# A router-gated expert layer and a two-way state scan on one core: two accumulations start from a ScalarE copy instead of an identity product

## The chip, the core and the metric

The kernel runs on one core of a Trainium2 chip. Its time is the device time of one execution in microseconds (us); the smaller, the better. The core has five instruction streams that run side by side and meet at semaphores: PE (TensorE, products into PSUM banks), DVE (VectorE), ACT (ScalarE), POOL (GpSimd) and SP (SyncE, here the queue that issues every transfer).

## What is computed

Eight images of 96 channels and 4096 pixels go through two layers, all in 32-bit floats. The reference, cut to what matters:

```python
# layer 0: four experts, two of them gated per pixel
gates = softmax(top2(tokens @ router_w.T + router_b))          # zero for the other two
for ei in range(4):
    hid = gelu(tokens @ fc1_w[ei].T + fc1_b[ei])
    out = out + gates[..., ei:ei + 1] * (hid @ fc2_w[ei].T + fc2_b[ei])
x2 = x + scale[0] * out

# layer 1: normalise over channels, then a selective scan over the pixels, forwards and backwards
x_norm = (x2 - mean) * rsqrt(var + 1e-5) * gamma + beta
def mamba(u):
    xr, z = split(u @ W_in);  xr = silu(conv4(xr) + conv_b)
    dt, B, C = split(xr @ W_xproj);  dt = softplus(dt @ W_dt + b_dt)
    h_t = exp(dt_t * A) * h_(t-1) + (dt_t * xr_t) * B_t        # 192 channels x 16 states
    y_t = sum_n(h_t * C_t) + xr * D
    return (y * silu(z)) @ W_out
out = 0.5 * (mamba(x_norm) + mamba(x_norm reversed) reversed) + x2
```

## The kernel before

**Tiling.** An image is cut into 8 chunks of 512 pixels. The 192 x 16 states of a chunk are 24 tiles of 128 rows, in six batches of four. After a setup, one *body* works on one chunk in one direction: 8 forward bodies and then 8 reverse ones for each image, 128 in all. The text calls them F0 to F7 and R0 to R7; R0 works on the last chunk again, from its right end. The even bodies also carry half of the expert layer's work of one piece (512 pixels) of the *next* image, the odd ones the other half.

**One body on the engines.** DVE runs 24 scans (line 1180, one for each tile, each on its factor exp(dt A)), four products with B (1164), the gated hidden tiles (1144, three of them, at scans 14, 15 and 16) and the products of the summed state with silu(z), called *gated y* below (1185). ACT computes the 24 factors (944) into a ring of three PSUM banks, two tiles ahead of DVE; so it can be at most three ahead. In between it has the softplus, gelu, silu and copy steps, at fixed tile numbers. POOL multiplies each scanned batch by C (1267) and two batches by B (1257). PE sums the states of each batch into the bank of y (`sum_states`, 710) and does all projections. Every engine's order is written out by hand in its `body`; nothing is reordered.

**The bank of y.** y is summed in one PSUM bank in two parts, *low* (batches 0 and 1) and *high* (batches 2 to 5). Each part opens with ACT writing xr D into the bank (`seed`, 949). In a reverse body PE then adds the forward y of the same chunk by a product with the identity (704, `y_begin`) and the result passes gate and output projection. The high sum of body n ends in body n + 1: PE there adds batches 4 and 5, and DVE takes the gated y (1185) ahead of its scan 6. The low one is taken at scan 13.

**The forward y** of a chunk is copied out of PSUM by ACT into `yf` (`evacuate`, 954), stored to memory (526) and loaded back into `yb` (531) for the reverse body. For R0 this is a round trip through memory directly after the forward pass: `yf` low is copied in F7, `yf` high at tile 5 of R0.

**The two sums that start from x.** "Y2" is the second expert layer's output in work bank 0: in an even body PE adds x by an identity product (652, `residual`) and six products with the hidden tiles (658) and three for the bias (662). "OUT" is the chunk's output in work bank 1: PE adds x2 by an identity product (719, `finish`) and two products with the gated y (720, 721). It happens one body after each reverse body, so in R1 to R7 and in F0 (`fin` in the code).

**SP's queue** is in order: a wait holds all issues behind it. In a body it waits for "D1" (the softplus input projection), loads the window of the chunk two ahead (439), the residual x2 (521), stores and loads B and C (451, 463, 470), stores and loads dt and dt x (445, 446, 476, 456, 481), and in an even body loads x of the next piece (423), for which it waits until Y2 is complete.

## Time and profile before

| what | value |
|---|---|
| median of 3 runs | 6012.41 us (5996.08 to 6017.89) |
| the profiled execution, its own time | 6026.74 us |
| its span, first instruction to last | 6024.9 us |
| DVE busy in it | 5274.0 us, 88% |
| POOL busy | 5153.9 us, 86% |
| PE busy | 4725.7 us, 78% |
| ACT busy | 4472.2 us, 74% |
| mean granted TensorE clock | 0.84 of full speed |

The first scan begins at 401.5 us and the last ends at 6007.2 us of the span, so a body takes 43.8 us in the mean; what comes before is the router, the gates and the first image's experts. No engine is saturated: DVE and POOL hand batches to each other and each waits for the other, and DVE waits for factors, for sums and for gate rows. So the profile is read body by body, where one begins at its first scan.

### The profile page before, as it was taken

The numbers are of one execution on the slowest core, as the hardware profiler recorded it, in microseconds if no ns is written. First come the engines' busy times: TensorE is split into PE (matmuls) and PEld (weight loads), VectorE is DVE, ScalarE is ACT, GpSimd is POOL, SyncE is SP. The second block draws the span as 40 slices with busy tenths as digits, with TensorE's granted clock in tenths as the row PEclk, the third lists the DMA queues.
The fourth block names the chain that finished last, engine by engine and source line by source line (L and its number), as shares of the span: only waits on it lengthen the run. The fifth ranks groups of instructions, "written<-read, shape, count | busy, mean of one in ns | idle before, by whom it ended". The sixth has DMA issues, their size and how long they took to land.

```text
span 6024.9 us, 68387 instructions
## 1 busy us (share of the span) xinstructions
PE 4725.7 (78%) x13769; PEld 1472.7 (24%) x13769; DVE 5274.0 (88%) x4473; ACT 4472.2 (74%) x6727; POOL 5153.9 (86%) x2127
## 2 busy tenths in 40 slices
PE   7767788777887778777787778777787778877787
PEld 7222222222222222222222222222222222222222
DVE  1239989998999989999899989999899998999898
ACT  0448877787777877778777877778777787778776
POOL 0039988999899989999899988999899998999898
PEclk9877788878887878877888788888888878887788
DMA  3046667676776766676676766666676766766776
GB/s 95 22 99 164 169 163 174 164 172 161 173 169 163 173 157 172 167 170 162 169 178 161 173 160 171 167 172 163 169 170 163 175 161 166 172 168 165 169 177 149
DMA packets 428352, 964.89 MB, mean 160 GB/s; under 512 B 58081, under 2 KB 58330, under 8 KB 394985
## 3 DMA queue, kind: packets, MB, share of 16 engines
q1 hardware_dynamic: 428008, 961.31, 65.4%
q14 instruction: 249, 2.03, 0.1%
q8 instruction: 95, 1.56, 0.1%
HBM read 776.98 MB, written 184.11 MB: 160 GB/s over the span
## 4 chain that ended last, share of the span: by engine, by line
issue 22%; DVE 19%; PE 18%; ACT 12%; DMA 11%; POOL 7%; SPq 2%; DVEq 1%; ACTq 1%; POOLq 0%
DVE X L1180 13%; PE ps L679 5%; DMA bc_d<-bc 4%; POOL X L1267 4%; DVE X L1164 4%; ACT ps L944 3%; PE ps L710 3%; POOL X L1257 2%; DMA lo_d<-bc 2%; DMA lo<-lo_d 2%; PE ps L658 2%; DVE hid L1144 2%; PE ps L694 1%; DMA y_d<-yf 1%; PE ps L684 1%
## 5 line engine op out<-in xcount | busy, mean ns | idle before, releaser
L1267 POOL TENSOR_TENSOR X<-X,cR 128x2048 f32<-128x2048 f32 x768 | 3477.8, 4528 | 61.7
L1180 DVE TENSOR_TENSOR_SCAN X<-ps,carry,X 128x512 f32<-128x512 f32 x2688 | 3258.5, 1260 | 113.3 <-ACT ps L944 91.5
L944 ACT ACTIVATE ps<-hi,amat 128x512 f32<-128x512 f32 x2048 | 1375.1, 682 | 688.0 <-DVE X L1180 684.6
L1164 DVE TENSOR_TENSOR X<-hi,ps 128x2048 f32<-128x2048 f32 x512 | 1158.9, 2264 | 85.2 <-PE ps L710 81.9
L710 PE MATMUL ps<-X,red 128*32 128x512 f32 x6144 | 918.0, 673 | 377.3 <-POOL X L1267 376.8
L1257 POOL TENSOR_TENSOR X<-lo,bR 128x2048 f32<-128x2048 f32 x258 | 1167.4, 4525 | 40.0 <-DMA lo<-lo_d 38.6
L679 PE MATMUL ps<-win,w_u 97*128 97x512 f32 (+1 forms) x2080 | 1118.5, 688 | 11.6 <-DMA win<-xn_d 8.6
L944 ACT ACTIVATE ps<-lo,amat 128x512 f32<-128x512 f32 x1026 | 687.3, 677 | 165.1 <-DVE X L1180 132.0
L694 PE MATMUL ps<-xr,wd 128*96 128x512 f32 (+1 forms) x520 | 417.8, 898 | 340.7 <-ACT xr L899 287.6
L642 PE MATMUL ps<-xp,w 96*128 96x512 f32 x864 | 534.2, 754 | 67.4 <-DMA xp<-in_x 67.1
L679 PEld LDWEIGHTS ps<-win,w_u 97*128 97x128 f32 (+1 forms) x2080 | 372.3, 190 | 652.2 <-issue 637.6
L1180 DVE TENSOR_TENSOR_SCAN X<-ps,X 128x512 f32<-128x512 f32 x384 | 445.3, 1202 | 38.3 <-POOL X L1257 18.9
L1144 DVE TENSOR_TENSOR hid<-ps,hid 128x512 f32<-128x512 f32 x432 | 287.4, 667 | 210.7 <-PE ps L649 210.1
L1265 POOL COPY carry<-X 128x4 f32<-128x4 f32 x768 | 143.2, 187 | 359.1 <-DVE X L1180 354.6
L658 PE MATMUL ps<-hid,w 128*96 128x512 f32 x852 | 421.3, 615 | 0.0
L710 PEld LDWEIGHTS ps<-X,red 128*32 128x32 f32 x6144 | 125.5, 112 | 1067.2 <-POOL X L1267 660.7
L695 PE MATMUL ps<-xr,wd 65*96 65x512 f32 (+1 forms) x520 | 373.2, 809 | 0.0
L1230 POOL TENSOR_TENSOR xnp<-xc,sq 96x512 f32<-96x512 f32 x71 | 90.1, 1269 | 330.5 <-ACT sq L892 330.5
L857 ACT ACT_TABLE_LOAD x265 | 340.0, 1283 | 4.7
L866 ACT ACTIVATE hid<-ps,b 128x512 f32<-128x512 f32 x432 | 273.3, 685 | 61.1 <-PE ps L642 59.0
L932 ACT ACTIVATE ps<-bR 128x512 f32<-128x512 f32 x512 | 298.1, 582 | 0.0
L642 PEld LDWEIGHTS ps<-xp,w 96*128 96x128 f32 x864 | 185.9, 234 | 413.5 <-issue 377.7
(112 smaller groups left out, 4291.9 us busy)
## 6 DMA issues: line engine op xcount, KB each, us to landing
hi<-hi_d SPq DMA_DIRECT2D x516, 512.0 KB, 8.5
bR<-bc_d SPq DMA_DIRECT2D x516, 256.0 KB, 4.5
lo<-lo_d SPq DMA_DIRECT2D x516, 256.0 KB, 4.6
cR<-bc_d SPq DMA_DIRECT2D x516, 256.0 KB, 6.9
hi_d<-S SPq DMA_DIRECT2D x258, 256.0 KB, 7.8
y_d<-yf SPq DMA_DIRECT2D x128, 256.0 KB, 8.4
yb<-y_d SPq DMA_DIRECT2D x128, 256.0 KB, 7.6
win<-xn_d SPq DMA_DIRECT2D x130, 196.3 KB
```

The costliest lines, as they stand in the source:

```text
L642: ready(u, f"H{m}", mm(begin(u, f"H{m}")[:, :], w1[:, P * m:P * m + P], xp[:, :], start=True, stop=True))
L658: mm(p_w[u.at["Y2"][0]][0:C, :], w2[:, m, :], hid[:, m, :], start=False, stop=False)
L679: last = mm(out[0:m, :], w_u[:, t, a:a + m], win[:, par, at:at + CH], start=(t == 0), stop=(t == TAPS - 1))
L694: mm(out[0:m, :], w_d[0][:, a:a + m], xr[0][:, par, :], start=True, stop=False)
L695: ready(u, name, mm(out[0:m, :], w_d[1][:, a:a + m], xr[1][0:DR + 1, par, :], start=False, stop=True))
L710: last = mm(p_y[GRP * j:GRP * j + GRP, :], red[:, :], X[:, slot(par, s), j, :], start=False, stop=(s in (LOW - 1, NB - 1)), skip_group_che ...
L944: A_(p_a[i % RING][:, :], dt, ACT.Exp, scale=amat[:, column(i):column(i) + 1]).then_inc(s_exp, 1)
L1144: free(u, f"G{m}", V.tensor_tensor(hid[:, m, :], begin(u, f"G{m}")[:, :], hid[:, m, :], ALU.mult))
L1164: V.tensor_tensor(X[:, slot(par, s), :, :], hi[:, par, HIGH:2 * HIGH, :], p_b[:, :].unsqueeze(1).to_broadcast([P, BATCH, CH]), ALU.mult).t ...
L1180: V.tensor_tensor_scan(h, a, h, 0.0 if head else carry[:, i:i + 1], ALU.mult, ALU.add).then_inc(s_scan, 1)
L1257: G.tensor_tensor(batch(par, s), lo[:, LOW:2 * LOW, :].unsqueeze(1).to_broadcast([P, 2, 2, CH]), quads(bR, par, s), ALU.mult).then_inc(s_b ...
L1267: G.tensor_tensor(batch(par, s), batch(par, s), quads(cR, par, s), ALU.mult).then_inc(s_hc, 1)
```

## The change

- `residual` is gone from the body (it stays in the setup loop). ACT writes x from `xp` into the bank of Y2 (`seed_x`) right behind its factor of tile 2, ahead of the softplus; the products with the hidden tiles accumulate onto it.
- The identity product of `finish` is gone but for the very last chunk. ACT writes x2 from `xf` into the bank of OUT (`seed_out`) at tile 6, behind the seed of y and ahead of the copy of Y2.
- In an even body PE sums the batches 4 and 5 of the body before directly behind one another, and the last three products of the second expert layer come behind both. Batch 2 is summed ahead of the second projection (`project(1)`), in even bodies only.
- R0 takes the forward y out of `yf`, where ACT wrote it, and the last chunk's two loads of `yb` are dropped. That chunk is still stored.
- SP's load of the next piece's x waits for `seed_x`, no longer for a complete Y2.

```diff
@@ SP @@
                 if not odd:
-                    bank, at = u.at["Y2"]
-                    wait_alone(s_pr[bank], at + 1)
+                    wait_alone(s_xs, pc - NCH + 1)
                     load_piece(nimg, j)
...
                 if before == 0:
                     store_y(0, n - 1, NCH - 1 if rev else q * 2 + odd - 1)
-                    if rev:
-                        load_y(0, (img + 1) * NCH, NCH - 1, n * NB + (LOW + 2))
...
-                if nrev:
-                    following = NCH - 1 if not rev else chunk_of(q, rev, odd) - 1
-                    load_y(1, (img + 1) * NCH, following, n * NB + (NB + 1))
+                if nrev and rev:
+                    load_y(1, (img + 1) * NCH, chunk_of(q, rev, odd) - 1, n * NB + (NB + 1))
@@ PE @@
-            def y_begin(low, n, f, par):
+            def y_begin(low, n, first, f, par):
                 pe.wait_ge(s_seed, n * 2 + (1 if low else 2))
-                if f is not None:
-                    pe.wait_ge(s_yl[low], f * 16 + 16)
-                    mm(p_y[:, :], ident[:, :], yb[:, low, :], start=False, stop=False, skip_group_check=True)
+                if f is not None or first:
+                    src = yf if first else yb
+                    if not first:
+                        pe.wait_ge(s_yl[low], f * 16)
+                    mm(p_y[:, :], ident[:, :], src[:, low, :], start=False, stop=False, skip_group_check=True)
...
                 pe.wait_ge(s_ev, n * 2 + 4)
-                pe.wait_ge(s_xf, f * 16 + 16)
-                out = begin(u, "OUT") if u is not None else p_b
-                mm(out[0:C, :], ident[0:C, 0:C], xf[:, :], start=True, stop=False)
+                if u is not None:
+                    out = begin(u, "OUT")
+                    pe.wait_ge(s_fs, f + 1)
+                else:
+                    out = p_b
+                    pe.wait_ge(s_xf, f * 16 + 16)
+                    mm(out[0:C, :], ident[0:C, 0:C], xf[:, :], start=True, stop=False, skip_group_check=True)
...
-                    residual(u)
+                    begin(u, "Y2")
+                    pe.wait_ge(s_xs, pc - NCH + 1)
                     for m in range(3):
                         expert_out(m, u, None)
                     if before is not None:
                         sum_states(n - 1, NB - 2, nxt)
-                    expert_out(3, u, None)
-                    expert_out(4, u, None)
-                    if before is not None:
                         sum_states(n - 1, NB - 1, nxt)
-                    expert_out(5, u, None)
+                    for m in range(3, HT):
+                        expert_out(m, u, None)
                     expert_bias(u)
-                y_begin(1, n, f, par)
+                y_begin(1, n, first, f, par)
...
-                y_begin(0, n, f, par)
+                y_begin(0, n, first, f, par)
+                if not odd:
+                    sum_states(n, 2, par)
                 project(1, par, urev, u)
-                sum_states(n, 2, par)
+                if odd:
+                    sum_states(n, 2, par)
@@ ACT @@
+            def seed_x(v, pc):
+                bank, at = v.at["Y2"]
+                act.wait_ge(s_pf[bank], at + 1)
+                act.wait_ge(s_xp, pc * 16)
+                A_(p_w[bank][0:C, :], xp[:, :], ACT.Copy).then_inc(s_xs, 1)
+
+            def seed_out(u, f):
+                bank, at = u.at["OUT"]
+                act.wait_ge(s_pf[bank], at + 1)
+                act.wait_ge(s_xf, f * 16 + 16)
+                A_(p_w[bank][0:C, :], xf[:, :], ACT.Copy).then_inc(s_fs, 1)
...
                     if i == 0:
+                        if not odd:
+                            seed_x(u, pc)
                         softplus_start(1, u, n + 1)
...
-                    if i == 6 and not odd:
-                        copy_x2(u, pc - 1)
+                    if i == 6:
+                        if before == 1:
+                            seed_out(u, finished(img, q, rev, odd)[2])
+                        if not odd:
+                            copy_x2(u, pc - 1)
```

PE at the head of the even bodies R2 and R4 (one loop), before: x by the identity, three hidden tiles, then the two late sums with two hidden tiles between them.

```order
L652 MATMUL ps<-xp,ident 96x512
L658 MATMUL ps<-hid,w 96x512 x3
...
L710 MATMUL ps<-X,red 32x512 x4
L658 MATMUL ps<-hid,w 96x512 x2
...
L710 MATMUL ps<-X,red 32x512 x4
L658 MATMUL ps<-hid,w 96x512
L662 MATMUL ps<-gT,b2s 96x512 x3
```

The same place of the changed kernel (lines shifted: 652 was the identity product, 656 is 658, 711 is 710, 660 is 662).

```order
L656 MATMUL ps<-hid,w 96x512 x3
L709 ISA
L711 MATMUL ps<-X,red 32x512 x4
L709 REGISTER_ALU
L711 MATMUL ps<-X,red 32x512 x4
L656 MATMUL ps<-hid,w 96x512 x3
L660 MATMUL ps<-gT,b2s 96x512 x3
```

The identity product is gone and the second late sum stands ahead of two hidden products that it stood behind.

SP between the last body of a forward pass and the loads of R0, before: the store of the low forward y (526) and its load (531) stand ahead of R0's window (439).

```order
L526 DMA y_d<-yf 128x512
L387 ISA
L387 REGISTER_ALU
L531 DMA yb<-y_d 128x512
L387 REGISTER_ALU
L439 ISA
L439 DMA win<-xn_d 97x518
L387 REGISTER_ALU
L451 DMA bc_d<-bc 32x512
```

And of the changed kernel (528 is 526, 441 is 439, 453 is 451).

```order
L528 DMA y_d<-yf 128x512
L389 REGISTER_ALU
L441 ISA
L441 DMA win<-xn_d 97x518
L389 REGISTER_ALU
L453 DMA bc_d<-bc 32x512
```

R0's window and its store of B and C are no longer behind a load that waits for a store to land.

## Rows read from the trace of the kernel before

**Rows 1.** The page's head: span, and busy time, share and instructions of each engine.

```profile
span 6024.9 us, 68387 instructions
PE 4725.7 (78%) x13769; PEld 1472.7 (24%) x13769; DVE 5274.0 (88%) x4473; ACT 4472.2 (74%) x6727; POOL 5153.9 (86%) x2127
```

**Rows 2.** Waits of DVE, whole span: who <- whom: us in total, times, longest.

```profile
DVE hid L1144 <- PE ps L649: 210.1, 86, 16.4
DVE yr L1185 <- PE ps L710: 128.6, 50, 9.3
DVE X L1180 <- ACT ps L944: 110.1, 137, 2.4
...
DVE X L1164 <- PE ps L710: 81.9, 61, 8.9
```

**Rows 3.** Sums over stretches: length, busy by engine, means. All R0; then R2, R4, R6.

```profile
sum 423.80, PE 342.47 PEld 100.50 DVE 316.81 ACT 289.00 POOL 331.11; mean PE 42.81 PEld 12.56 DVE 39.60 ACT 36.12 POOL 41.39
...
sum 1089.80, PE 989.21 PEld 303.89 DVE 996.96 ACT 862.64 POOL 963.09; mean PE 41.22 PEld 12.66 DVE 41.54 ACT 35.94 POOL 40.13
```

**Rows 4.** Timeline of R0, image 5: start, us, what [idle before it <- who ended it].

```profile
3549.59 0.27 SPq L439 DMA_DIRECT2D win<-xn_d  x1
...
3559.90 1.71 SPq L463 DMA_DIRECT2D bR<-bc_d  x4
...
3563.17 0.34 SPq L423 DMA_DIRECT2D xp<-in_x  x1
...
3569.18 4.53 PE L642 MATMUL ps<-xp,w 96*128 96x512 f32 x6 [4.01 <-DMA xp<-in_x]
...
3574.78 0.69 DVE L1185 TENSOR_TENSOR yr<-ps,sz 128x512 f32<-128x512 f32 x1 [4.50 <-PE ps L710]
...
3585.80 2.05 PE L704 MATMUL ps<-yb,ident 128*128 128x512 f32 x2 [6.61 <-DMA yb<-y_d]
...
3593.77 2.29 DVE L1164 TENSOR_TENSOR X<-hi,ps 128x2048 f32<-128x2048 f32 x1 [7.61 <-PE ps L710]
```

**Rows 5.** Waits of PE for transfers, whole span.

```profile
PE ps L642 <- DMA xp<-in_x: 67.1, 31, 6.6
...
PE ps L704 <- DMA yb<-y_d: 41.1, 8, 6.6
```

**Rows 6.** Timeline at the head of R4, image 4, whose first scan is at 3032.4.

```profile
3033.57 4.55 POOL L1267 TENSOR_TENSOR X<-X,cR 128x2048 f32<-128x2048 f32 x1
...
3035.64 1.10 PE L652 MATMUL ps<-xp,ident 96*96 96x512 f32 x2
...
3040.25 1.96 PE L658 MATMUL ps<-hid,w 128*96 128x512 f32 x4
3042.13 1.07 PE L710 MATMUL ps<-X,red 128*32 128x512 f32 x8
...
3043.27 0.69 DVE L1185 TENSOR_TENSOR yr<-ps,sz 128x512 f32<-128x512 f32 x1 [2.54 <-PE ps L710]
```

**Rows 7.** Stretches: R2 and R4 of image 5 (length, busy, granted clock, DMA, GB/s).

```profile
3645.60:3691.30 45.70, 38.86 (x109) 11.75 (x108) 41.36 (x36) 36.00 (x55) 41.41 (x18) 0.87 0.69 170
3734.80:3778.30 43.50, 37.55 (x110) 11.48 (x109) 41.42 (x36) 35.88 (x55) 41.34 (x18) 0.92 0.72 182
```

**Rows 8.** PE and DVE in these two bodies, timeline.

```profile
3664.13 4.18 PE L642 MATMUL ps<-xp,w 96*128 96x512 f32 x6 [1.84 <-DMA xp<-in_x]
...
3669.68 0.69 DVE L1185 TENSOR_TENSOR yr<-ps,sz 128x512 f32<-128x512 f32 x1 [2.54 <-PE ps L710]
...
3752.60 2.84 PE L642 MATMUL ps<-xp,w 96*128 96x512 f32 x6 [1.14 <-DMA xp<-in_x]
...
3756.50 0.69 DVE L1185 TENSOR_TENSOR yr<-ps,sz 128x512 f32<-128x512 f32 x1 [0.19 <-PE ps L710]
```

**Rows 9.** ACT and DVE at the head of R4, image 4, timeline.

```profile
3037.71 2.44 DVE L1180 TENSOR_TENSOR_SCAN X<-ps,carry,X 128x512 f32<-128x512 f32 x2
...
3038.02 0.67 ACT L944 ACTIVATE ps<-lo,amat 128x512 f32<-128x512 f32 x1
```

**Rows 10.** Group by shape: busy, mean ns | idle. Then a transfer: KB, median us.

```profile
L932 ACT ACTIVATE ps<-bR 128x512 f32<-128x512 f32 x512 | 298.1, 582 | 0.0
...
xf<-x_d SPq DMA_DIRECT2D x64, 192.0 KB, 10.1
```

More of the change, by code:

```diff
@@ L340, in moe_mamba @@
         s_seed = sem("y_seeded")
+        s_xs = sem("x_seeded")
+        s_fs = sem("residual_seeded")
         s_ys = [sem("forward_y_high_stored"), sem("forward_y_low_stored")]
@@ L591, in _ @@
                 sp.wait_ge(s_win[k], 16 * (IMGS * BODIES // 2 + 1))
-                sp.wait_ge(s_yl[k], 16 * NCH * IMGS)
+                sp.wait_ge(s_yl[k], 16 * (NCH - 1) * IMGS)
             for replicated in (s_lo, s_hi, s_b, s_c):
@@ L651, in residual @@
             def residual(u):
[L652 removed]
+                mm(begin(u, "Y2")[0:C, :], ident[0:C, 0:C], xp[:, :], start=True, stop=False, skip_group_check=True)
             def expert_out(m, u, gu):
@@ L657, in expert_out @@
                     pe.wait_ge(s_pf[bank], at + 2)
-                mm(p_w[u.at["Y2"][0]][0:C, :], w2[:, m, :], hid[:, m, :], start=False, stop=False)
+                mm(p_w[u.at["Y2"][0]][0:C, :], w2[:, m, :], hid[:, m, :], start=False, stop=False, skip_group_check=True)
             def expert_bias(u):
                 for s in range(3):
-                    last = mm(p_w[u.at["Y2"][0]][0:C, :], b2s[:, s, :], gT[:, :], start=False, stop=(s == 2))
+                    last = mm(p_w[u.at["Y2"][0]][0:C, :], b2s[:, s, :], gT[:, :], start=False, stop=(s == 2), skip_group_check=True)
                 ready(u, "Y2", last)
@@ L716, in finish @@
                 pe.wait_ge(s_ev, n * 2 + 4)
-                pe.wait_ge(s_xf, f * 16 + 16)
-                out = begin(u, "OUT") if u is not None else p_b
-                mm(out[0:C, :], ident[0:C, 0:C], xf[:, :], start=True, stop=False)
-                mm(out[0:C, :], wo0[:, :], yr0[:, :], start=False, stop=False)
-                last = mm(out[0:C, :], wo1[:, :], yr1[:, par, :], start=False, stop=True)
+                if u is not None:
[5 more added lines that the diff above has]
+                    mm(out[0:C, :], ident[0:C, 0:C], xf[:, :], start=True, stop=False, skip_group_check=True)
+                mm(out[0:C, :], wo0[:, :], yr0[:, :], start=False, stop=False, skip_group_check=True)
+                last = mm(out[0:C, :], wo1[:, :], yr1[:, par, :], start=False, stop=True, skip_group_check=True)
                 if u is not None:
@@ L771, in body @@
                 nimg = next_image(img)
-                f = img * NCH + q * 2 + odd if rev else None
+                first = rev == 1 and before == 0
+                f = img * (NCH - 1) + q * 2 + odd if rev and not first else None
                 windows = (img * (BODIES // 2) + q + ((NCH // 2) * rev + 2)) * 16
```

1 line of the change is left out of this document (removed).

## The prediction

> **What bounds the kernel now.** I read the page's head first [rows 1]: DVE is busy 88% and POOL 86%, so neither is full and the time lies in what DVE waits for. The waits of DVE [rows 2] name three that the change touches: the gated y waits for PE's sums (128.6 us in 50 times), the product with B waits for PE to have summed the slot that it overwrites (81.9 in 61), the gated hidden tile waits for a gate row (210.1 in 86). Then I cut the span into bodies and summed them by kind [rows 3]. The 8 bodies R0 take 423.8 / 8 = 53.0 us each, and DVE works in 39.6 of them: 13.4 us idle. The 24 bodies R2, R4 and R6 take 1089.8 / 24 = 45.4 each with 41.5 of work: 3.9 idle. The mean body is 43.8. R0 is the outlier, and its timeline [rows 4] shows why in two places. PE stands 4.01 us for x of the next piece, and DVE then 4.50 for the low sum behind it. Then PE stands 6.61 us for the forward y on its way through memory, runs its product at half speed (2.05 us), and DVE waits 7.61. The waits of PE [rows 5] hold 8 such waits for yb, 41.1 us: one for each image. In the even reverse bodies it is the high sum [rows 6]: DVE waits 2.54 us for it at the gated y, while POOL's last product of the old body had ended at 3033.57 + 4.55 = 3038.12, 4 us before PE came to sum it at 3042.13. PE is late there, by its own work.
>
> **The change part by part.**
>
> *R0's forward y from `yf`.* PE's product at 3585.80 no longer waits: its data lie in SBUF from tile 5 of the body on, and the seed that it also needs waits for no transfer. DVE's 7.61 us go. Over the 8 images PE waited 5.1 in the mean and 6.61 here, while DVE waited 1.0 more than PE; that bounds DVE's mean by 6.1 and 7.6, and the longest wait of this kind is 8.9 [rows 2, 5]. I take 7.0: 8 x 7.0 = 56 us. What is late next is ACT: behind its silu steps the factors come late, in 110.1 / 137 = 0.8 us a time [rows 2], a wait that R0 now meets as the other reverse bodies do: 8 x 0.8 = 6 back. Net **-50 us**, bounds -40 and -60. Batch 2 is also summed ahead of the second projection; the slot is then free earlier, but ACT's silu is what DVE waits for next, so this counts nothing.
>
> *R0's two loads and their waits on SP.* A load of yb that had to wait for its store stood ahead of R0's window. From the window's issue to the landing of B and C's store, which lets 463 go, it is 3559.90 - 3549.59 = 10.3 us, and x of the next piece is issued 3.3 us behind that and comes 6.0 us later [rows 4]. So as much as the window moves forward, x does, and DVE's 4.50 shrinks by that. No row shows how long SP stood for the store; the bounds are 0 and PE's 4.0 us. I take 1.5, nearer to the lower one since the projection that frees the window ends late too: 8 x 1.5 = **-12 us**, bounds 0 and -32.
>
> *Even reverse bodies: the identity product of x, and the sum moved ahead.* On PE's path to the high sum the change takes out 1.10 us (652) and puts 1.96 us (658) behind it: 3.06 us. The sum would end at 3043.20 - 3.06 = 3040.14, and DVE is there at 3043.27 - 2.54 = 3040.73 [rows 6]. The wait of 2.54 goes wholly. What is late next can be seen in two bodies of image 5 in which PE happened to come early and the gated y had no wait at tile 6: R4 took 43.5 us and R2 took 45.7 [rows 7]. In both PE then stood for x of the next piece. In R4 it was 1.14 us, the six products took 2.84, and the low sum cost DVE 0.19. In R2 it was 1.84 us, the products took 4.18, part of them at the lower clock, and DVE waited 2.54 for the low sum: the whole gain was lost one step on [rows 8]. So a body is worth between -0.3 (45.4 - 45.7) and +1.9 us (45.4 - 43.5). SP issues the load of x behind the stores of dt, not behind Y2, so its new wait moves nothing, and x lands as late as before. PE comes there another 1.0 us earlier, since the identity product of x2 is gone as well, which makes its stand longer. I take three bodies of R4's sort for one of R2's: (3 x 1.9 - 0.3) / 4 = 1.35.
>
> *The copies on ACT.* Their price: the copy SBUF to PSUM of 512 columns is 582 ns [rows 10]. At the head of a body ACT is dense. Scan 5 starts at 3037.71 + 1.22 = 3038.93 and its factor is ready at 3038.69 [rows 9]: 0.24 us of cover, so of the 0.58 of `seed_x` 0.34 lands on DVE. That leaves 1.0 in an even reverse body: 24 x 1.0 = **-24 us**, bounds -46 and +15 (45.7 + 0.34 - 45.4 = 0.64 each). The store of B and C is 0.58 us later too, but it lands behind the window and the residual (10.1 us) anyway. In F2, F4 and F6 the 0.34 has no gain beside it, and waits for gate rows at tile 14 hide a part: 0 to 0.34, I take 0.3: 24 x 0.3 = **+7 us**. `seed_out` stands at tile 6, behind the seed of y; the residual comes 10.1 us after its issue [rows 10], which is about when ACT gets there, so ACT may stand up to 1 us. Queued behind it are the copy of Y2 and the factor of tile 9, and PE's products of OUT wait for it; DVE has a product with B (2.3 us, rows 4) and three scans of 1.2 ahead of that tile. I count nothing.
>
> *F0 and the odd bodies.* F0 loses its own wait for the high sum, and as in R2 of image 5 I expect x to give it back one step on: 0, bounds -1 and +1 a body (8 us either way). Odd reverse bodies have one product less (1.0 us) in a stretch in which PE waits for POOL: 0.
>
> *Sum:* 50 + 12 + 24 - 7 = 79 us. The profiled execution took 6026.7 and would take 5948; the median of the runs is 14 us lower, 6012.4, so the **forecast is 5933 us**, 1.3% faster.
>
> **The rivals.**
>
> *Everything lands* (0.15). x is early enough everywhere and the clock holds: R0 8 x (7.6 + 4.0) = 93, even reverse bodies 24 x 1.9 = 46: 139 us, 5873. For it: in R4 of image 5 it was so. Against it: R2 of the same image, and that nothing brings x earlier outside R0.
>
> *Only R0's round trip pays* (0.12). The even reverse bodies trade the wait for the high sum for one for the low sum, and `seed_x` costs 0.34 us in all 56 other even bodies: 50 - 19 = 31 us, 5981. For it: R2 of image 5.
>
> *R0 pays by half* (0.07). With yb gone something else holds its second half, the high dt loads or ACT: 8 x 3.5 = 28 in place of 50, 5955.
>
> *TensorE at the lower clock; slower than before* (0.04). With two products out of its dense stretch PE idles longer ahead of the products with x. The granted clock was 0.92 in R4 and 0.87 in R2 of image 5, and the difference of these bodies is 45.7 - 43.5 = 2.2 us. If every even body goes R2's way, the 24 reverse ones lose 0.64 each (15 us) and the 32 forward ones 2.2 (70 us), against 50 from R0: 6012 + 35 = 6047. [...]
> The Trainium skill, "TensorE: Matmul & The Clock Gate", section "What's actually happening", says that the lower clock is the default state and activity releases it: a rule against taking products out of PE. By it alone the result would be the 6047 of this rival instead of 5933; the two bodies agree with its direction, and no row shows that all bodies would follow.
>
> **How the numbers follow.** The forecast has 0.62: its own range is 5905 to 5960. The rivals have 0.15, 0.12, 0.07 and 0.04. The range to hold 8 of 10 takes in most of the first and the second: 5880 to 5985. A measurement of this kernel can tell some 0.5% from no change, that is 30 us: faster below 5982, slower above 6042. Faster: 0.62 + 0.15 + 0.07 + half of 0.12 = 0.90; the other half of the second and a part of the last are within: 0.07; slower 0.03.
>
> **What the changed profile would show.** R0 near 44.5 us (from 53.0) with no wait of PE for yb, and DVE's wait for the low sum there at 3 us in place of 4 to 5. The gated y at tile 6 without a wait in R2, R4, R6 and F0. PE's wait for x longer in total than 67.1 us, in more than 31 places. The even reverse bodies in two sorts again, near 44 and near 46. DVE waiting for factors about 0.3 us at scan 5 of even bodies. The prediction is wrong if R0 stays above 48, if the bodies R2 to R6 stay at 45.4, or if the forward ones grow by over 1 us.

## The result, and the profile after

The changed kernel took 5920.86 us in the median of four runs (5911.16 to 5929.55), the kernel before 6014.51 beside it (5996.08 to 6017.89): a ratio of 0.985, interval 0.9825 to 0.9876. The forecast was 5933. The profiled execution has a span of 5920.9 us against 6024.9.

Line numbers move: the scan is 1208 (was 1180), the gated y 1213 (1185), the product with B 1192 (1164), the gated hidden tile 1172 (1144), the factor 967 (944), PE's sums 711 (710), its products with x of the next piece 640 (642). The waits of DVE over the whole span (who <- whom: us in total, times, longest), beside [rows 2]:

```profile
DVE hid L1172 <- PE ps L647: 213.0, 95, 17.3
DVE X L1208 <- ACT ps L967: 136.0, 164, 2.0
...
DVE yr L1213 <- PE ps L711: 74.1, 32, 9.3
...
DVE X L1192 <- PE ps L711: 10.4, 28, 0.4
```

The gated y fell from 128.6 to 74.1 us and the product with B from 81.9 to 10.4; waits for factors rose from 110.1 to 136.0. Of PE's two rows of waits for transfers in [rows 5] one is left (yb is gone), and it has grown from 67.1 us in 31 places:

```profile
PE ps L640 <- DMA xp<-in_x: 102.7, 61, 6.9
```

R0 of image 5, beside [rows 4]: SP's issues of the window, of B and C's store, of their load and of x, then PE's products with x, then the two waits of DVE of over 1 us that are left.

```profile
3492.99 0.26 SPq L441 DMA_DIRECT2D win<-xn_d  x1
3497.70 0.31 SPq L453 DMA_DIRECT2D bc_d<-bc  x1
3503.13 1.69 SPq L465 DMA_DIRECT2D bR<-bc_d  x4
...
3506.71 0.34 SPq L425 DMA_DIRECT2D xp<-in_x  x1
...
3512.00 5.49 PE L640 MATMUL ps<-xp,w 96*128 96x512 f32 x6 [3.26 <-DMA xp<-in_x]
...
3519.42 0.69 DVE L1213 TENSOR_TENSOR yr<-ps,sz 128x512 f32<-128x512 f32 x1 [4.67 <-PE ps L711]
...
3537.87 2.34 DVE L1208 TENSOR_TENSOR_SCAN X<-ps,X 128x512 f32<-128x512 f32 x2 [1.52 <-ACT ps L967]
```

The 7.61 us at the second product with B are gone; x is issued 12.8 us into the body (3506.71 - 3493.91) in place of 13.6, and DVE's 4.67 us for the low sum stand as before. In this image 5 is the exception. Over all eight R0, x is issued 13.1 us into the body in the mean in place of 14.7, and DVE's waits for the low sum add up to 30.4 us in place of 42.2. R0 of image 4, before and then changed:

```profile
2877.67 0.69 DVE L1185 TENSOR_TENSOR yr<-ps,sz 128x512 f32<-128x512 f32 x1 [7.02 <-PE ps L710]
...
2832.21 0.69 DVE L1213 TENSOR_TENSOR yr<-ps,sz 128x512 f32<-128x512 f32 x1 [3.49 <-PE ps L711]
```

Summed by kinds of bodies (a view of stretches: length, busy by engine, means): R0; then R2, R4, R6; then F2, F4, F6 and the odd forward bodies, and after them these last two of the kernel before.

```profile
sum 360.30, PE 308.31 PEld 93.55 DVE 315.44 ACT 291.96 POOL 320.42; mean PE 38.54 PEld 11.69 DVE 39.43 ACT 36.50 POOL 40.05
...
sum 1073.20, PE 934.44 PEld 282.77 DVE 995.81 ACT 887.17 POOL 978.25; mean PE 38.93 PEld 11.78 DVE 41.49 ACT 36.97 POOL 40.76
...
sum 988.10, PE 756.13 PEld 233.96 DVE 964.38 ACT 857.13 POOL 904.94; mean PE 31.51 PEld 9.75 DVE 40.18 ACT 35.71 POOL 37.71
...
sum 1376.00, PE 998.21 PEld 265.54 DVE 1289.23 ACT 1049.79 POOL 1353.69; mean PE 31.19 PEld 8.30 DVE 40.29 ACT 32.81 POOL 42.30
```

```profile
sum 1025.00, PE 832.10 PEld 252.83 DVE 967.02 ACT 850.03 POOL 943.70; mean PE 34.67 PEld 10.53 DVE 40.29 ACT 35.42 POOL 39.32
...
sum 1349.40, PE 964.89 PEld 258.50 DVE 1286.10 ACT 1046.80 POOL 1310.09; mean PE 30.15 PEld 8.08 DVE 40.19 ACT 32.71 POOL 40.94
```

With the sums of the other kinds from the same view:

| kind (count) | before | after | difference | forecast |
|---|---|---|---|---|
| R0 (8) | 423.8 | 360.3 | -63.5 | -62 |
| R2, R4, R6 (24) | 1089.8 | 1073.2 | -16.6 | -24 |
| R odd (32) | 1366.4 | 1359.1 | -7.3 | 0 |
| F0 (8) | 351.3 | 346.2 | -5.1 | 0 |
| F2, F4, F6 (24) | 1025.0 | 988.1 | -36.9 | +7 |
| F odd (32) | 1349.4 | 1376.0 | +26.6 | 0 |

So the reverse half went as forecast (-87 against -86). In the forward half two large differences that were not forecast nearly cancel (-15 in all).

The even reverse bodies R2, R4 and R6 come in two sorts, and the clock tells them apart. In 13 of the 24 PE's six products with x ran at a granted clock of 1.00 throughout (2.84 us); these bodies take 42.9 to 44.7 us, 43.8 in the mean. In 11 the clock over the products was 0.62 to 0.75 (3.70 to 4.49 us), so they ran in part at the lower level; these take 45.4 to 46.4, 45.8 in the mean. Before the change it was 1 of 24. R4 and R6 of image 5, which take 43.3 and 45.6 us, PE and then the stretch of its products:

```profile
3689.22 2.84 PE L640 MATMUL ps<-xp,w 96*128 96x512 f32 x6 [1.69 <-DMA xp<-in_x]
3689.20:3692.10 2.90, 2.88 (x10) 1.17 (x14) 2.90 (x3) 2.87 (x5) 0.73 (x3) 1.00 0.78 194
...
3775.34 3.90 PE L640 MATMUL ps<-xp,w 96*128 96x512 f32 x6 [1.78 <-DMA xp<-in_x]
3775.30:3779.20 3.90, 3.86 (x10) 1.24 (x12) 3.52 (x3) 3.27 (x5) 1.73 (x3) 0.71 0.91 214
```

The length of the stand ahead does not sort them by itself: PE had stood 0.14 to 2.37 us in the bodies at 1.00 and 1.56 to 2.58 us in the others.

The experiments ask what carries each part.

### The profile page after: what moved, and what is told of

Its sections match the earlier page's. It is cut to its first block, busy times and chain, and to the rows that moved or that the text cites. A ratio compares the mean times of both kernels' runs of the same rounds, so it can differ in the third digit from the quotient of the medians.

```text
span 5920.9 us, 68105 instructions
## 1 busy us (share of the span) xinstructions
PE 4658.8 (79%) x13515; PEld 1447.1 (24%) x13515; DVE 5270.1 (89%) x4473; ACT 4531.7 (77%) x6854; POOL 5155.7 (87%) x2127
## 4 chain that ended last, share of the span: by engine, by line
issue 23%; DVE 21%; PE 14%; DMA 12%; ACT 11%; POOL 7%; SPq 3%; DVEq 1%; ACTq 1%; POOLq 0%
DVE X L1208 14%; DMA bc_d<-bc 5%; PE ps L677 4%; DVE X L1192 4%; POOL X L1295 4%; ACT ps L967 3%; POOL X L1285 2%; DMA lo<-lo_d 2%; DMA xp<-in_x 2%; PE ps L711 2%; DMA lo_d<-bc 2%; PE ps L640 2%; DVE hid L1172 2%; PE ps L682 2%; SPq L465 1%
## 5 line engine op out<-in xcount | busy, mean ns | idle before, releaser
L1295 POOL TENSOR_TENSOR X<-X,cR 128x2048 f32<-128x2048 f32 x768 | 3477.9, 4529 | 62.2 <-POOL carry L1293 0.7
L1192 DVE TENSOR_TENSOR X<-hi,ps 128x2048 f32<-128x2048 f32 x512 | 1158.3, 2262 | 10.4 <-PE ps L711 10.4
L711 PE MATMUL ps<-X,red 128*32 128x512 f32 x6144 | 900.2, 666 | 334.1 <-POOL X L1295 331.0
L692 PE MATMUL ps<-xr,wd 128*96 128x512 f32 (+1 forms) x520 | 451.7, 967 | 334.4 <-ACT xr L922 281.3
L640 PE MATMUL ps<-xp,w 96*128 96x512 f32 x864 | 528.7, 746 | 104.2 <-DMA xp<-in_x 102.7
L1172 DVE TENSOR_TENSOR hid<-ps,hid 128x512 f32<-128x512 f32 x432 | 288.2, 669 | 213.4 <-PE ps L647 213.0
L693 PE MATMUL ps<-xr,wd 65*96 65x512 f32 (+1 forms) x520 | 400.3, 864 | 0.0
L682 PE MATMUL ps<-win,w_g 97*128 97x512 f32 x256 | 177.2, 780 | 156.0 <-ACT xr L922 156.0
```

What stands on the lines that cost most here:

```text
L640: ready(u, f"H{m}", mm(begin(u, f"H{m}")[:, :], w1[:, P * m:P * m + P], xp[:, :], start=True, stop=True))
L692: mm(out[0:m, :], w_d[0][:, a:a + m], xr[0][:, par, :], start=True, stop=False)
L693: ready(u, name, mm(out[0:m, :], w_d[1][:, a:a + m], xr[1][0:DR + 1, par, :], start=False, stop=True))
L711: last = mm(p_y[GRP * j:GRP * j + GRP, :], red[:, :], X[:, slot(par, s), j, :], start=False, stop=(s in (LOW - 1, NB - 1)), skip_group_che ...
L1172: free(u, f"G{m}", V.tensor_tensor(hid[:, m, :], begin(u, f"G{m}")[:, :], hid[:, m, :], ALU.mult))
L1192: V.tensor_tensor(X[:, slot(par, s), :, :], hi[:, par, HIGH:2 * HIGH, :], p_b[:, :].unsqueeze(1).to_broadcast([P, BATCH, CH]), ALU.mult).t ...
```

## The experiments

In the table, ratios are to the kernel before, run on the same chip each time; body lengths are from one profile each (sum of the kind by its count), and "forward" is the sum of all 64 forward bodies. A difference of under 1 us in the column of R2, R4 and R6 need not come from the edit: e8_pool touches forward bodies alone, and that column rose from 44.7 to 45.7.

| kernel | ratio (95%) | R0 | R2, 4, 6 | R odd | forward |
|---|---|---|---|---|---|
| before | 1 | 53.0 | 45.4 | 42.7 | 2726 |
| changed | 0.985 (0.9825 to 0.9876) | 45.0 | 44.7 | 42.5 | 2710 |
| e1_yf | 0.9894 (0.9868 to 0.992) | 45.7 | 44.6 | 42.9 | 2722 |
| e2_sums | 0.999 (0.998 to 1.0) | 52.2 | 44.5 | 43.0 | 2726 |
| e3_no_seed_x | 0.9858 (0.9829 to 0.9886) | 45.5 | 44.8 | 42.4 | 2721 |
| e4_no_seed_out | 0.9878 (0.9861 to 0.9894) | 46.3 | 44.4 | 43.2 | 2713 |
| e5_sum2_back | 0.988 (0.9857 to 0.9903) | 45.1 | 45.4 | 42.5 | 2723 |
| e6_x_early | 0.9785 (0.9765 to 0.9806) | 42.2 | 44.2 | 42.7 | 2706 |
| e7_fill | 0.9836 (0.9813 to 0.986) | 43.4 | 45.1 | 42.5 | 2726 |
| e8_pool | 0.986 (0.9835 to 0.9884) | 45.2 | 45.7 | 42.5 | 2701 |
| e9_pe_x | 0.9798 (0.9782 to 0.9814) | 42.6 | 44.2 | 42.5 | 2722 |
| e10_no_copies | 0.9844 (0.9827 to 0.986) | 43.8 | 44.7 | 43.0 | 2719 |
| e11_pe_x_pool | 0.9784 (0.9768 to 0.9801) | 42.5 | 44.1 | 42.5 | 2709 |
| e12_residual_first | 0.9923 (0.9909 to 0.9937) | 42.6 | 43.7 | 44.5 | 2736 |

**e1_yf: R0's forward y alone**

```diff
-                    if rev:
-                        load_y(0, (img + 1) * NCH, NCH - 1, n * NB + (LOW + 2))
...
-                    mm(p_y[:, :], ident[:, :], yb[:, low, :], start=False, ...)
+                    src = yf if first else yb
+                    mm(p_y[:, :], ident[:, :], src[:, low, :], start=False, ...)
```

> The kernel before with one part of the change alone: in R0 the forward y comes from yf, and the two loads of yb that R0 had per image are gone. Nothing else is touched. Theory A (the prediction's first two terms): R0 falls from 53.0 us to about 45 as in the changed kernel, 8 x 7.8 = 62 us, all other kinds of bodies stay within 0.3 us of the kernel before: 6014 - 62 = 5952. Rival B (R0's fall in the changed kernel also needs the earlier high sum and x2 out of PE): R0 stays at 47 or above, gain below 48 us, above 5966. Rival C (what R0 gains is handed to its neighbours): R0 near 45, R1 longer by 1 us or more.

Measured 5954 against 6024: 70 us, Theory A (forecast 5952). This one part is some 1.1 of the change's 1.5%. R0 lost 7.2 us. R2, R4 and R6 fell too, by 0.8 us each, to where the whole change has them, with both identity products and the old order of sums still in place. That was not expected by any theory. The waits left in them are not those of the changed kernel: DVE still waits for the high sum in 13 of these 24 bodies, 31.8 us in all (20 and 54.6 before, none in the changed kernel), and the clock over the products with x falls in 2 of them (11 in the changed kernel). That both have the same mean is not shown to have one cause.

**e2_sums: batch 5 summed directly behind batch 4, alone**

```diff
-                    expert_out(3, u, None)
-                    expert_out(4, u, None)
-                    if before is not None:
                         sum_states(n - 1, NB - 1, nxt)
-                    expert_out(5, u, None)
+                    for m in range(3, HT):
+                        expert_out(m, u, None)
```

> The kernel before with PE's sum of the last batch (5) put directly behind that of batch 4 in even bodies, ahead of products 3 and 4 of the second expert layer; both identity products stay on PE. By the trace of before that moves the high sum 1.96 us earlier. Theory A (the place of the sum carries what the change gains in even bodies outside R0): F2, F4 and F6 fall by 1.0 to 1.5 us a body (24 to 36 us), the even reverse bodies by 0.5 to 0.7 (12 to 17), the odd forward bodies grow by 0.5 to 0.8 (16 to 26) since POOL sets the length of a forward pair, and all in all 15 to 30 us go: 5985 to 6000. Rival B (the product taken out of PE carries it): less than 8 us, above 6006, and the wait of DVE at the gated y of tile 6 stays in more than half of the even bodies.

A miss for Theory A in time: 0.999. (The table's row flatters it: the profiled run, 6010 us, is one of the fastest of ten, which took 6009 to 6027.) The high sum does come earlier, and its wait goes from 128.6 us to 68.8, but the product with B takes most of it back: 81.9 became 100.6, and 3.1 us for ACT's copies of B became 20.2:

```profile
DVE X L1162 <- PE ps L710: 100.6, 75, 9.1
...
DVE yr L1183 <- PE ps L710: 68.8, 31, 9.3
...
DVE X L1162 <- ACT ps L930: 20.2, 30, 1.0
```

**e3_no_seed_x and e4_no_seed_out: one copy each undone**

```diff
e3 @@ PE, ACT @@
-                    begin(u, "Y2")
-                    pe.wait_ge(s_xs, pc - NCH + 1)
+                    residual(u)
-                        if not odd:
-                            seed_x(u, pc)
e4 @@ PE, ACT @@
-                    out = begin(u, "OUT")
-                    pe.wait_ge(s_fs, f + 1)
+                pe.wait_ge(s_xf, f * 16 + 16)
+                mm(out[0:C, :], ident[0:C, 0:C], xf[:, :], start=True, ...)
-                        if before == 1:
-                            seed_out(u, finished(img, q, rev, odd)[2])
```

> The changed kernel with x brought into the bank of the second expert layer by PE's identity product again, and ScalarE's copy of x and the waits for it taken out; all else as changed. Theory A (the copy costs ACT 0.58 us ahead of the factors and buys PE 1.1 us which it then stands for x of the next piece): a draw, within 12 us of the changed kernel's 5921, with DVE's waits for factors down from 136 us to about 118 and a wait for the high sum of at most 1 us at tile 6 of even bodies. Rival B (the 1.1 us of PE are on the path): slower than the changed kernel by 25 to 60 us (56 even bodies x 0.5 to 1.0), 5946 to 5981. Rival C (the copy only costs): faster than it by 12 to 20 us, 5901 to 5909.

> The changed kernel with the residual brought into the bank of the output by PE's identity product again and ScalarE's copy of it taken out; all else as changed. Theory A (the prediction counted this part at nothing): within 10 us of the changed kernel's 5921. Rival B (PE's shorter way to x of the next piece is worth something): slower by 15 to 40 us, with PE's wait for x shorter than the changed kernel's 102.7 us by 20 us or more. Rival C (a longer stand for x costs clock): faster by 10 to 30 us, for the same shorter wait.

e3 also puts SP's old wait for a complete Y2 back ahead of the load of x. It is the draw of its Theory A in time, 0.9858 against 0.985, within the intervals (its detail is wrong: the waits for factors rose from 136.0 to 148.9 us). The copy of x moves time between the forward bodies: without it F2, F4 and F6 are back at 42.6 us (1021.7 / 24; 41.2 with it) and the odd ones at 42.1 (1348.4 / 32; 43.0 with it).

e4 is slower by 0.28%, 17 us. The intervals overlap (0.9861 to 0.9894 and 0.9825 to 0.9876), so the size rests on e10_no_copies below, where the same edit is clear of noise. Size and mark are those of Rival B (PE's wait for x is 67.7 us, 35 less), but its mechanism is not: the even reverse bodies, where PE stood for x, are no longer for it (44.4; 44.7 in the changed kernel). The extra time is in the odd reverse bodies (1381.7 against 1359.1). R1 of image 5 shows the chain: PE, then ACT, then DVE.

```profile
3566.72 2.07 PE L705 MATMUL ps<-yb,ident 128*128 128x512 f32 x2 [3.46 <-ACT ps L967]
3568.58 1.91 PE L720 MATMUL ps<-xf,ident 96*96 96x512 f32 x2
3570.29 1.92 PE L721 MATMUL ps<-yr,wo 128*96 128x512 f32 x2
...
3573.29 0.60 ACT L902 ACTIVATE xf<-ps 96x512 f32<-96x512 f32 x1 [2.31 <-PE ps L722]
3573.78 0.59 ACT L950 ACTIVATE ps<-bR 128x512 f32<-128x512 f32 x1
...
3574.49 2.29 DVE L1185 TENSOR_TENSOR X<-hi,ps 128x2048 f32<-128x2048 f32 x1 [0.72 <-ACT ps L950]
...
3592.44 2.29 DVE L1185 TENSOR_TENSOR X<-hi,ps 128x2048 f32<-128x2048 f32 x1 [1.43 <-PE ps L711]
```

After a stand of 3.46 us PE's granted clock is 0.50, so that the identity product of the residual costs 1.7 to 1.9 us there and not 1.1. OUT is late by it, ACT stands 2.31 us at the copy of OUT, ACT's next copy of B is queued behind, and DVE waits for that copy (0.72), then for a sum (1.43). Over the 32 odd reverse bodies ACT stands 64.4 us at this copy (35.4 in the changed kernel) and DVE 42.4 us at the product with B (none). In the changed kernel ACT's stand at this place is 1.10 us and both waits of DVE are gone:

```profile
3555.41 0.60 ACT L907 ACTIVATE xf<-ps 96x512 f32<-96x512 f32 x1 [1.10 <-PE ps L727]
3555.90 0.59 ACT L955 ACTIVATE ps<-bR 128x512 f32<-128x512 f32 x1
```

These are the waits that also ate e2's gain. That the earlier sum pays only where OUT is short fits both, but no run has the earlier sum and `seed_out` without the rest.

**e5_sum2_back: batch 2 summed behind the second projection again**

```diff
-                if not odd:
-                    sum_states(n, 2, par)
...
-                if odd:
-                    sum_states(n, 2, par)
+                sum_states(n, 2, par)
```

> The changed kernel with the sum of batch 2 put back behind the second projection in even bodies; all else as changed. Theory A (the prediction counted this move at nothing): within 10 us of the changed kernel (0.983 to 0.987 of the kernel before). Rival B (its slot comes free too late for DVE's product with B at tile 19): DVE's wait at the product with B up from 10.4 us by 20 us or more (56 even bodies x 0.4 to 1.4) and the time by as much.

0.988: 0.3% above the changed kernel, but their intervals overlap (0.9857 to 0.9903 and 0.9825 to 0.9876), so this is inconclusive. Rival B's mark is absent: the wait at the product with B is 12.6 us (10.4). What grew is the gated y, from 74.1 to 99.6: the clock over the products with x is below 1.00 in 17 of the 24 even reverse bodies in place of 11, and those 17 take 46.2 us in the mean, the other 7 take 43.5. That is the whole growth of these bodies (45.4 from 44.7); why more of them fell is open.

**e6_x_early: x of the next piece issued ahead of yb and B**

```diff
                 store_bc(n + 1, nxt)
+                if not odd:
+                    wait_alone(s_xs, pc - NCH + 1)
+                    load_piece(nimg, j)
                 if fin and rev:
...
-                if not odd:
-                    wait_alone(s_xs, pc - NCH + 1)
-                    load_piece(nimg, j)
```

> The changed kernel with one more edit: SyncE issues the load of x of the next piece directly behind the store of B and C, ahead of the loads of yb and of B and of the low dt store, in even bodies. Theory A (the low sum of the even reverse bodies is late because PE stands for x, 102.7 us in 61 places): PE's wait for x falls below 40 us, DVE's wait at the gated y of tile 13 (64.9 us in all) below 25, R0 to about 42 and the other even reverse bodies to 43.3: 8 x 3 + 24 x 1.3 = 55 us less, 0.976 of the kernel before. Rival B (the loads that it now stands ahead of are as urgent): the wait moves to B or to the dt tiles and the time stays within 0.5% of the changed kernel. Rival C (x can only be taken once PE has read the piece ahead of it, and it is issued at once already): the issue moves by under 1 us and nothing changes.

Theory A in direction, and 0.9785 against its 0.976. By its ratio the changed kernel would take 6028 x 0.985 = 5937 us here; e6_x_early took 5895, 42 us less (55 were expected). PE's wait for x:

```profile
PE ps L639 <- DMA xp<-in_x: 1.8, 1, 1.8
```

102.7 us have become 1.8, and the clock over the products with x is 1.00 in R0 and in all 24 even reverse bodies. R0 is at 42.2 and R2, R4 and R6 at 44.2, not the 43.3 expected: DVE's waits for factors rose from 136.0 to 168.7 us. One part of the gain is single: F0 of image 1 took 50.8 us in the changed kernel and 42.7 here.

**e7_fill: two filler products ahead of PE's wait for x**

```diff
+                    fill = begin(u, "H0")
+                    for _ in range(2):
+                        mm(fill[:, :], w1[:, 0:P], w1[:, 0:CH], start=True, stop=True)
```

> The changed kernel with two filler products of constant data (their result is overwritten) put on PE ahead of its wait for x in even bodies: added work only. Theory A (PE's stand for x lowers the granted clock, and that makes the slow sort of the even reverse bodies): that sort is gone, the even reverse bodies fall from 44.7 to about 43.5, 24 x 1.2 = 29 us less, in spite of 2 x 0.2 to 0.5 us more work a body. Rival B (the slow sort comes from x's arrival and from the order alone): no change or up to 30 us more, with the products of the hidden tiles behind the filler as slow as before.

Neither in full. The clock over the products with x is 1.00 in all 24 even reverse bodies, and yet R2, R4 and R6 did not gain (45.1; 43.7 to 46.4). The run does not isolate the clock: x landed 1.1 us later in them in the mean (in R2 19.0 to 20.6 us into the body, 18.4 to 19.1 in the changed kernel). In R0, where PE's stand is longest, the effect is plain: R0 fell from 45.0 to 43.4. Image 5, PE in e7_fill; beside it the products with x in the changed kernel took 5.49 us after a stand of 3.26 (above):

```profile
3523.89 1.88 PE L812 MATMUL ps<-w 96*128 96x512 f32 x4
...
3526.61 2.84 PE L640 MATMUL ps<-xp,w 96*128 96x512 f32 x6 [0.84 <-DMA xp<-in_x]
```

The granted clock over these six products is the number behind the busy times, 1.00 of full speed (2.4 GHz) here and 0.50 (1.2 GHz) in the changed kernel:

```profile
3526.60:3529.50 2.90, 2.89 (x10) 1.18 (x14) 2.57 (x3) 2.87 (x5) 1.19 (x2) 1.00 0.75 187
```

```profile
3512.00:3517.50 5.50, 5.50 (x10) 1.93 (x14) 2.75 (x3) 2.88 (x4) 3.62 (x2) 0.50 0.94 210
```

Over all eight R0 DVE's waits for the low sum fell from 30.4 to 13.8 us: work that nobody needs made R0 1.6 us shorter. In all, e7_fill is 0.9836 against 0.985, within the intervals.

**e8_pool: two groups of POOL's work cut to 16 of 512 columns in forward bodies, the rest left out**

```diff
-                times_x(1, u, nxt)
+                times_x(1, u, nxt, CH if rev else 16)
-                    normalise(pc - 1)
+                    normalise(pc - 1, CH if rev else 16)
```

> The changed kernel with less work on POOL in forward bodies: the multiplication that makes the normalised piece (1.26 us, once a pair of bodies) and the one that makes dt*x of the low rows (1.27 us, twice a pair) take 16 columns of 512 there, the rest of both tiles is left as it was, so that part of the computation is left out. In all some 3.5 us of POOL a forward pair are gone and nothing on another engine. Theory A (POOL sets the length of a forward pair; that is why all six kernels so far have 83.7 to 84.3 us for a pair from F2 on, whatever they gained in its even body): a pair gets shorter by 1.5 us or more, 32 pairs x 1.5 to 3 = 50 to 95 us, and DVE's waits for gate rows at tiles 14 and 16 shrink below half of 68 us. Rival B (POOL's load only looks like the bound, DVE's own chain sets it): under 15 us.

A clear miss for Theory A: the two groups of POOL's work went from 164.4 to 97.1 and from 90.0 to 56.7 us, 100.6 us less, and the ratio is 0.986. The waits for gate rows did shrink (213.0 to 177.2), and the odd forward bodies fell from 43.0 to 41.6 us (1330.4 / 32), but F2, F4 and F6 rose from 41.2 to 42.6 (1022.5 / 24):

```profile
DVE X L1208 <- ACT ps L967: 185.8, 184, 5.9
DVE hid L1172 <- PE ps L647: 177.2, 63, 16.5
```

Waits for factors went from 136.0 to 185.8. ACT around tile 14 of F4, image 5, and the scan that waits for it:

```profile
3358.25 1.28 ACT L875 ACT_TABLE_LOAD   x1
3359.54 1.84 ACT L875 ACTIVATE hid<-ps,b 128x512 f32<-128x512 f32 x3
3361.40 1.28 ACT L866 ACT_TABLE_LOAD   x1
3362.70 0.69 ACT L967 ACTIVATE ps<-hi,amat 128x512 f32<-128x512 f32 x1
...
3363.42 1.28 DVE L1208 TENSOR_TENSOR_SCAN X<-ps,carry,X 128x512 f32<-128x512 f32 x1 [1.45 <-ACT ps L967]
```

Two table loads and three gelu steps are 4.4 us in which no factor is made. ACT can be only three factors ahead, so a DVE that comes faster out of the odd body meets this in the even one. F4 and F5 together keep their length by it (83.3 us; 83.6 in the changed kernel). This is not all that hides the gain. F2 and F3 together fell from 83.5 to 81.9 and the forward half by 9 us, while R2, R4 and R6, which the edit does not touch, took 23 us more (1096.2 against 1073.2), with the clock below 1.00 in 16 of the 24 in place of 11. So in the forward half the relief bought 9 us for 100.6 of work.

**e9_pe_x, e10_no_copies, e11_pe_x_pool: on top of the early x**

```diff
e9 @@ e6_x_early with x by PE, which now lets the next x be loaded @@
-                    begin(u, "Y2")
-                    pe.wait_ge(s_xs, pc - NCH + 1)
+                    residual(u).then_inc(s_xs, 1)
-                        if not odd:
-                            seed_x(u, pc)
e10 @@ e9 with e4's edit @@
e11 @@ e9 with e8's edit @@
```

> The kernel with the early load of x (e6_x_early, 0.9785 of the kernel before), with x brought into the bank by PE's identity product again in place of ScalarE's copy; the product itself gives the signal that lets x of the next piece be loaded, so the load stays early. Theory A (with x early, PE has room at the head of even bodies and ScalarE has not: DVE's largest wait in e6_x_early is for factors, 168.7 us, above all at tile 14 of even bodies): the factor waits fall by 56 x 0.3 to 0.6 = 17 to 34 us and the kernel takes 0.973 to 0.976. Rival B (PE's 1.1 us more ahead of the high sum come back as a wait at tile 6, as before the change): 0.980 to 0.985. Rival C (one cancels the other, as in the pair e3_no_seed_x and the changed kernel): 0.977 to 0.980.

> As e9_pe_x, and the residual too is brought in by PE's identity product: no copy of the change is left on ScalarE, and what remains of it is the forward y taken from yf, the order of the sums and the freed gate on x. Theory A (the copy of the residual shortens the way PE - ScalarE's copy of the output - ScalarE's next copy of B, which DVE waits for at tile 11 of odd reverse bodies, and PE's sum behind it at tile 19): slower than e9_pe_x by 0.2 to 0.4%, with R1 at 43.8 and R7 at 42.4 again, as in e4_no_seed_out. Rival B (with x early it no longer matters): equal to e9_pe_x within 0.1%.

> As e9_pe_x, with POOL's work in forward bodies cut as in e8_pool (the normalised piece and dt*x of the low rows on 16 columns of 512 there: part of the computation is left out). In e8_pool the odd forward bodies fell by 2.1 us (42.6 to 40.6) and the even ones grew by 1.8, with DVE's waits for ScalarE's factors at tiles 10 and 14 in place of those for gate rows. Theory A (a forward pair is held by POOL in its odd body and by ScalarE in its even one, and only relief of both shortens it): the pair F4 and F5 falls below 82.5 us (83.6 in the changed kernel, 83.4 in e8_pool) and the kernel takes 20 to 45 us less than e9_pe_x. Rival B (DVE's own work of 80.5 us a pair and short waits are the floor): the pair stays at 83 or above, within 15 us of e9_pe_x.

e9, 0.9798, is at the edge of Rival C (a draw; expected 0.977 to 0.980): also with x early, the copy of x on ACT cannot be told from nothing (0.9782 to 0.9814 without it, 0.9765 to 0.9806 with it), and the waits for factors did not fall without it (172.4 us; 168.7 with it). e10 is Theory A: 0.9844, 0.46% or 28 us above e9, with R odd at 43.0 again. The two intervals are apart, so the copy of the residual is worth that much with x early; without, e4_no_seed_out gave 0.28%. e11 is Rival B: 0.9784, 6 to 8 us below e9. The odd forward bodies fell to 41.6 and the even ones rose to 43.0 (1031.4 / 24), as in e8. With POOL relieved in every forward body and ACT free of one copy a pair, F4 and F5 together keep their length (83.3; 83.4 in e9), and F2 and F3 lose 1.3 us (83.4; 84.7).

**e12_residual_first: the residual loaded ahead of the window**

```diff
+                if fin:
+                    load_residual(*finished(img, q, rev, odd))
                 if last and rev:
                     load_window(nimg, odd, ...)
...
-                if fin:
-                    load_residual(*finished(img, q, rev, odd))
                 store_bc(n + 1, nxt)
```

> The kernel with the early load of x (e6_x_early, 0.9785 of the kernel before), with SyncE's load of the residual issued ahead of the load of the window in place of behind it. In e6_x_early the residual comes 10 us after its issue, and ScalarE stands 54.6 us in all at its copy of it, with the factors and B's copy queued behind. Theory A (those 10 us are the window's transfer, which it queues behind, and ScalarE's stand is on the path): the residual comes 5 us sooner, ScalarE's stand goes, R2 and R4 fall by 0.3 to 0.8 us, and the kernel takes 0.973 to 0.977. Rival B (ScalarE catches up before a factor is late): the stand goes and the time stays within 0.1% of 0.9785. Rival C (its wait for the store of the last output now holds the window, and the projection comes late): 0.980 or more, with PE waiting at the projection and R bodies longer.

Rival C, and far worse than it said: 0.9923. Theory A's own mark is all there: ACT stood no more for the residual, and R2, R4 and R6 were the shortest of all kernels (43.7). But SP stood for the store of the last output, 172.2 us (51.4 in e6_x_early), with everything behind it. In R3 of image 5, whose first scan is at 3643.78, SP's queue was:

```profile
3647.89 0.34 SPq L523 DMA_DIRECT2D xf<-x_d  x1
3648.49 0.24 SPq L441 DMA_DIRECT2D win<-xn_d  x1
3648.92 0.62 SPq L453 DMA_DIRECT2D bc_d<-bc  x1
...
3659.36 0.78 SPq L465 DMA_DIRECT2D bR<-bc_d  x2
```

and in R3 of e6_x_early, from 3609.66 on:

```profile
3609.49 0.27 SPq L441 DMA_DIRECT2D win<-xn_d  x1
3610.78 0.32 SPq L523 DMA_DIRECT2D xf<-x_d  x1
3612.93 0.31 SPq L453 DMA_DIRECT2D bc_d<-bc  x1
...
3621.25 2.87 SPq L465 DMA_DIRECT2D bR<-bc_d  x4
```

The load of B starts 15.6 us into the body in place of 11.6, and the loads of dt behind it are late too. POOL's waits for the low dt, in e12_residual_first and then in e6_x_early:

```profile
POOL X L1284 <- DMA lo<-lo_d: 125.6, 68, 12.9
```

```profile
POOL X L1284 <- DMA lo<-lo_d: 41.6, 36, 13.1
```

POOL's waits lie mostly in R2, R4 and R6 (56.0 us; 6.9 in e6_x_early), and DVE then waits for the high sum at the head of R3, R5 and R7 (62.2 us; 3.9). So the odd reverse bodies went from 42.7 to 44.5 us: not by a late window (it is issued 4.7 us into this R3, but PE waits for a window no more often than in e6_x_early, once), but by what stood behind it.

## Why the prediction was right, and where it was not

*R0's forward y (net -50) and the window (-12)*: -63.5 measured, and term by term over the eight R0 the forecast holds. DVE's waits at the product with B, the 7.61 us of image 5, go from 56.9 us to nothing (forecast 56), its waits for factors rise by 7.0 (forecast 6), and its waits for the low sum fall by 11.8 (forecast 12), with x issued 1.5 us sooner (the 1.5 that the text had taken between its bounds). That the 1.5 came out is luck in part, since nothing was read for it; the trace of before has SP's waits for the stores of the forward y, 141.8 us in 16 places, and they are gone. The mark that the wait in R0 would be 3 us was too low: it is 3.8 in the mean, from 5.3. e1_yf alone gives -57.9 of the -63.5. The rival that R0 pays by half fell.

*Even reverse bodies (-24)*: -16.6 measured. "The wait of 2.54 goes wholly" held: no gated y waits at tile 6 any more (54.6 us before); what is late next is the low sum behind x, as the prediction said. The prices of the two sorts held too: 43.8 and 45.8 us, where the text gives 43.5 and 45.7, and 0.34 more with `seed_x`. The step that failed is the share, "three bodies of R4's sort for one of R2's". It was 13 to 11: (13 x 1.6 - 11 x 0.4) / 24 = 0.7 us a body in place of 1.0. The text had named what raises that share, the longer stand for x once x2's product is gone too, and e4_no_seed_out shows it: with that product back PE's stands for x in these bodies fall from 39.4 us to 7.9 and none has a clock below 1.00. The parts do not add: e1_yf has 44.6 us in these bodies without either edit to which the 24 us were booked, and e2_sums 44.5. Why R0's repair alone shortens bodies two to six places later was not settled. With x early (44.2 in e6_x_early) DVE's waits here are for factors.

*The copies on ACT*: `seed_x` at 0.34 us on DVE's path was about right at scan 5 (0.28 a body), but "F2, F4, F6: +7 us" had the wrong sign, -36.9, and "odd bodies: 0" missed +26.6. The step that failed treats a body as independent. From F4 to F7 what the even one of a pair gains the odd one gives back: F4 and F5 together took 82.9 to 84.0 us in all kernels here and F6 and F7 84.0 to 84.7, while F4 and F5 singly moved between 40.2 and 43.1. F2 and F3 kept no such length (81.9 to 85.4), and their fall from 85.4 to 83.5 in the change is 15 us, all that the forward half lost; what shortened them is open. `seed_out` "I count nothing" was the other miss: it is worth 0.46% with x early (e10_no_copies against e9_pe_x), and some 0.28% without, within the intervals, by ACT's copy of OUT and the copy of B queued behind it. The text had named that queue's entries, but not the copy of B.

*The rival that TensorE falls to the lower clock and the kernel is slower* did not come: the mean granted clock went from 0.84 to 0.83 and the time down. Its mechanism exists: in 11 even reverse bodies the lower clock came with 2.0 us more a body, 22 us in all, where the text's own rows had it once. How much of this the clock itself costs is not shown, since e7_fill took the lower clock away there and gained nothing. In R0, where the clock was low before the change too (0.62 over the products in image 5), e7_fill shows 1.6 us, 8 times in the kernel. The Trainium skill's page "TensorE: Matmul & The Clock Gate", section "What's actually happening", which has the lower clock as the default that activity releases, is in line with the pair of rows in e7_fill; what a run gives back here is 13 us in R0, not the whole gain.

*The marks.* Right: R0 near 44.5 (45.0), no wait for yb, none at tile 6, two sorts near 44 and 46, PE's wait for x longer and in more places, 0.3 us at scan 5. Wrong: the low sum in R0 at 3 us. The odd forward bodies grew by 0.8 us, just inside the bound of 1 that the text had set for calling itself wrong.

*The total* is 5921 against 5933: 94 us gained where 79 were forecast. That it is so near is luck in part. In the forward half two misses, of some 44 us down and 27 up, nearly cancel, and the even reverse bodies miss by 7 the other way.

*The best version* is e6_x_early: 0.9785, 5895 us.

**Open:** what fixes the length of a forward pair (neither POOL's load alone, nor with `seed_x` off ACT; the gelu stretch and its two table loads are the candidate, and were not tried), what shortens F2 and F3, what makes the clock fall in one even reverse body and not in another, and the fall of R2 to R6 in e1_yf.

## What to carry to other kernels

When a wait in one body is removed, look at the pair or ring that the body belongs to before booking the gain: here F4 and F5 together kept their length to within 1.1 us in all fourteen kernels. A product dropped from PE paid where an in-order queue on another engine stood behind its result (copy of OUT, then copy of B), and nothing that the runs can tell where none did (x), whether PE then stood for a transfer (e3_no_seed_x) or not (e9_pe_x). Moving that one transfer ahead in SP's queue gained 0.65%, as much as both copies together (0.59%, e10_no_copies against e6_x_early). A transfer that must wait belongs behind those that need not: put first, it cost 1.4%.

## What the runs showed of the hardware

The same six products of 512 columns took 5.49 us at a granted clock of 0.50 after a stand of 3.26 us, and 2.84 us at 1.00 when two filler products (four entries of PE, 1.88 us) came ahead of a stand of 0.84 us. The granted clock can also fall behind shorter stands: over the same products it was 0.62 to 0.75 in 11 even reverse bodies after stands of 1.56 to 2.58 us, and 1.00 in others after up to 2.37 us. Issued earlier, x took longer to land (5.9 us in the median against 4.4 in the changed kernel); it then has the window and the residual under way beside it, and that this is the reason was not tested. Issued ahead of the window, the residual came in 2.5 us in the median in place of 10.0.
